# A second landing buffer for the sign-weight chunks at the start of a three-layer transformer kernel

## What is computed

```
Wb = sign(W_ffn)                                   # [1024, 1024]
x = x + 0.5 * einsum('bsi,oi->bso', layernorm(x), Wb)
x = x + linear_attention(layernorm(x))             # phi(t) = elu(t) + 1, 16 heads of 64
x = x + 0.5 * einsum('bsi,oi->bso', layernorm(x), Wb)
```

## Time and profile before

| | us |
|---|---|
| median of 2 runs | 2100.75 (2100.37 to 2101.12) |
| the profiled execution's own time | 2100.6 |
| span of its slowest core (core 3), first to last instruction | 2099.0 |
| spans of all eight cores | 2093.1 to 2099.0 |
| PE busy on core 3 | 1767.8 (84%) |
| ACT busy | 1233.5 (59%) |
| DVE busy | 759.8 (36%) |

### The profile page before, as it was taken

How to read it: one execution, slowest core, us unless ns; L and a number is a source line. 1 busy time by engine, 2 the same in 40 slices (tenths; PEclk the granted TensorE clock), 3 DMA queues, 4 the chain that set the end, 5 groups by cost and what they waited for, 6 DMA issues and landing times.

```text
span 2099.0 us, 33066 instructions; the slowest of 8 cores (2093.1 to 2099.0 us)
## 1 busy us (share of the span) xinstructions
PE 1767.8 (84%) x10784; PEld 793.0 (38%) x10784; DVE 759.8 (36%) x2049; ACT 1233.5 (59%) x2025; POOL 147.5 (7%) x274
## 2 busy tenths in 40 slices
PE   0289989989989989989899899778888888888887
PEld 0133333333333333333333333344444444444443
DVE  2033333333333333333333333134443443443443
ACT  1266766776766776766777766634444444444443
POOL 1000000000000001000000000011011011011010
PEclk9999999999999999999999999989999999999999
DMA  8612222222222223222222221123333333333332
GB/s 169 131 61 70 85 88 72 84 88 78 77 88 72 84 87 111 75 88 66 88 89 66 88 89 56 60 92 112 125 120 113 119 125 115 113 118 115 120 126 76
DMA packets 134630, 199.34 MB, mean 95 GB/s; under 512 B 88384, under 2 KB 88384, under 8 KB 134464
## 3 DMA queue, kind: packets, MB, share of 16 engines
q0 software_dynamic: 32960, 109.08, 16.0%
q1 hardware_dynamic: 101504, 88.15, 13.8%
HBM read 104.87 MB, written 83.89 MB: 90 GB/s over the span
## 4 chain that ended last, share of the span: by engine, by line
PE 54%; ACT 25%; issue 10%; DVE 6%; DMA 3%; ACTq 1%; DVEq 0%; SPq 0%
PE pA L463 34%; PE pA L474 12%; DVE y2t L341 4%; ACT u1b L442 3%; PE pA L468 3%; DMA stg<-wfT 3%; ACT mnb L397 3%; ACT mxb L399 3%; ACT u2b L448 3%; PE pA L478 2%; ACT nb L357 2%; ACT kbQ L385 2%; ACT eb L398 2%; PE tpB L453 2%; ACT kbQ L386 1%
## 5 line engine op out<-in xcount | busy, mean ns | idle before, releaser
L474 PE MATMUL pA<-wv,u1fm 128*128 128x512 bf16 x1024 | 245.3, 383 | 96.8 <-ACT kbK L401 96.8
L463 PE MATMUL pA<-sw,u2fm 128*128 128x512 bf16 x1024 | 234.6, 383 | 76.7 <-DVE y2t L341 75.5
L474 PE MATMUL pA<-wk,u1fm 128*128 128x512 bf16 x1024 | 242.4, 379 | 18.3 <-ACT kbQ L385 18.3
L442 ACT ACTIVATE u1b<-y2t 128x1024 bf16<-128x1024 f32 x64 | 67.6, 1057 | 299.5 <-DVE y2t L341 299.5
L463 PE MATMUL pA<-wo,attnfm 128*128 128x512 bf16 x1024 | 234.1, 382 | 4.9 <-DVE y3t L321 1.0
L463 PE MATMUL pA<-sw,u0fm 128*128 128x512 bf16 x1024 | 235.7, 384 | 0.0
L463 PE MATMUL pA<-wq,u1fm 128*128 128x512 bf16 x1024 | 232.1, 380 | 0.0
L474 PEld LDWEIGHTS pA<-wv,u1fm 128*128 128x128 bf16 x1024 | 90.9, 98 | 213.4 <-issue 123.8
L463 PEld LDWEIGHTS pA<-sw,u2fm 128*128 128x128 bf16 x1024 | 96.5, 98 | 194.7 <-issue 90.7
L382 ACT ACTIVATE u2b<-y1t 128x1024 bf16<-128x1024 f32 x63 | 66.6, 1057 | 175.9 <-DVE y1t L281 175.8
L312 DVE TENSOR_TENSOR phiQ<-eb,mxb 128x1024 bf16<-128x1024 bf16 x64 | 44.3, 693 | 344.0 <-ACT mxb L399 344.0
(11 more groups left out here) (119 smaller groups left out, 2418.1 us busy)
## 6 DMA issues: line engine op xcount, KB each, us to landing
xt<-x SPq DMA_DIRECT2D x64, 512.0 KB, 3.9
y1scr<-y1t POOLq DMA_DIRECT2D x64, 512.0 KB, 3.9
y1in<-y1scr POOLq DMA_DIRECT2D x64, 512.0 KB, 3.9
out<-y3t SPq DMA_DIRECT2D x64, 512.0 KB, 2.6
qscr<-qfm POOLq DMA_DIRECT2D x64, 256.0 KB, 3.2
qfin<-qscr POOLq DMA_DIRECT2D x64, 256.0 KB, 4.1
qfm<-phiQ SPq DMA_TRANSPOSE x512, 2.3
stg<-wfT SPq DMA_DIRECT2D x8, 512.0 KB, 8.6
```

The costliest lines, as they stand in the source:

```text
L442: e.activation(u1b[:, 0, :], y2t[:, tw % 2, :], AF.Square, accum_out=sq3b[:, :]).then_inc(sSq3, 1)
L463: mm = e.matmul(dst[:, h*512:(h+1)*512], lhs_fm[:, c*P:(c+1)*P], w_sb[:, c, h*512:(h+1)*512], start=(c == 0), stop=(last and c == 7))
L474: mm = e.matmul(dst[:, h*512:(h+1)*512], lhs_fm[:, c*P:(c+1)*P], w_sb[:, c, h*512:(h+1)*512], start=(c == 0), stop=(last and c == 7))
```

## The change

Chunks with an even number still land in `stg`, those with an odd number in `y3t[:, 0, :]`, which nothing else uses in this stage. SP's wait on `sSw` becomes c - 1 instead of c and begins at c = 2, so the buffer's last reader but one must be done. The wait on `gStg` is not changed: chunk c is issued only after chunk c - 1 has landed. ACT reads the buffer that fits.

```diff
             for c in range(8):
+                buf = stg[:, 0, :] if c % 2 == 0 else y3t[:, 0, :]
+                if c >= 2:
+                    e.wait_ge(sSw, c - 1)
                 if c >= 1:
-                    e.wait_ge(sSw, c)
                     e.wait_ge(gStg, 16 * c)
-                e.dma_start(out=stg[:, 0, :], in_=wfT[c*P:(c+1)*P, :]).then_inc(gStg, 16)
+                e.dma_start(out=buf, in_=wfT[c*P:(c+1)*P, :]).then_inc(gStg, 16)
@@
             for c in range(8):
                 e.wait_ge(gStg, 16 * (c + 1))
-                e.sign(sw[:, c, :], stg[:, 0, :]).then_inc(sSw, 1)
+                e.sign(sw[:, c, :], stg[:, 0, :] if c % 2 == 0 else y3t[:, 0, :]).then_inc(sSw, 1)
```

## The result

The changed kernel takes 2086.84 us (median), the kernel before 2101.4 us measured beside it. The ratio is 0.993, with a 95% interval of 0.9919 to 0.9941: 14.6 us less. The forecast was 2086 us in a range of 2081.5 to 2095.

What follows compares the result with a forecast made beforehand. Bound: eight serial `wfT` chunk loads ahead of PE's first work. Gaps 9.4 us, plus 6.1 for one slow transfer made fast, less a 0.5 tail, give 15.0 off 2100.6: 2086 us, range 2081.5 to 2095.

Steps and rivals of the forecast that it cites:

- Part 1: Gaps between chunk loads: ACT's sign no longer delays the next issue; gaps fall from 10.12 to 0.7 us, gain 9.4.
- Part 2: Start of the chunk loads: c2 gets in ahead of the weight loads, 6.1 us gained less a 0.5 us tail.
- Part 3: Chunks c3 to c7: c3 takes 11.21 us, the others 8.18 to 8.70; c7 lands at 66.8 us.
- Parts 4 to 6: Behind the chunks: no weight becomes the bound, the rest shifts as a block, core 4 ends last at 2084.3 us.
- The low stretch: PE's first tile: granted clock 0.62 over 97 to 106 us follows PE's pause; falling otherwise, at most 3.4 us either way.
- B: Rival: c2 does not get in ahead of the weight loads and takes 11.21 us; only gaps go, 2091 us; chance 0.14.
- C: Rival: full DMA engines stretch the transfers when gaps go, old cadence holds from c3; gain 9.2, 2091 us; chance 0.13.
- D: Rival: the shift makes granted-clock dips fall in three more slices, loss 20.4 us, 2106 us; chance 0.04.
- E: Rival: nothing happens, 2100.6 us, since the sign was not what held SP back; chance 0.05 shared with B with C.

Runs made afterwards that it cites:

- late_c3c7: Changed kernel with the new sign wait for c3 to c7 only, c1 and c2 keeping the old wait; ratio to the kernel before 0.9978.
- after_sign2b: Changed kernel with each chunk's sign taken twice, the second after the first; ratio to the kernel before 0.9939.
- before_hold3: Kernel before, with POOL's four weight loads held back until c2 has landed; ratio to the kernel before 0.9964.
- after_hold4: Changed kernel with the weight loads held until c3 has landed; ratio to the kernel before 0.9877.
- two_in_flight: Changed kernel without the wait for the landing just before, one landing semaphore per buffer, two transfers under way; 2065.47 us, ratio to the kernel before 0.9832.
- two_hold8: Changed kernel with two transfers under way and the weight loads held until all eight chunks have landed; 2071.38 us, ratio to the kernel before 0.9856.
- after_hold8: Changed kernel with the weight loads held until all eight chunks have landed; 2075.86 us, ratio to the kernel before 0.9882.

## Why the prediction was right

*What bounds.* Right: the eight chunks in series set PE's start, and what is behind shifts as a block (2013 to 2019 us before and after).

*Part 1, the sign leaves the cycle, 9.4 us.* Right. The semaphore's way to SP, taken as 0.1 us, is 0.07 to 0.08, so the seven gaps take 0.5 us where 0.7 were forecast. The half change late_c3c7 shows five of the seven gaps as 6.4 us against 5.8 expected, and after_sign2b shows that the sign has cover to spare.

*Part 2, c2 gets in ahead, 5.6 us.* Right, with c2 at 3.73 us against the 4.19 taken (3.69 and a tail of 0.5). The forecast said landing at 21.36 us; core 7's is at 21.45. That it is so near is in part luck: the tail of 0.5 us on c2 did not come, but c1 took 4.42 us where 3.69 were taken, and nothing on record says why. before_hold3 shows the mechanism by itself. One term failed in this step: "its bias loads are a few KB and share with one chunk before and after, so I leave 18.35 for `wq`". They are a few KB, but they go one after the other, beside the chunks, and on four cores they delay `wq` to 20.9 to 21.8 us. On those a second chunk is saved. It did not spoil the time, since the metric is the slowest core and the four others issue `wq` at 18.5 to 19.0; that some core stays without the delay was not part of the forecast. With the wait of after_hold4 on all cores the ratio is 0.9877. It does show in the mean, where the eighth sign is 17.0 us earlier and not 14 to 15.

*Part 3, the others keep their lengths.* Right on the whole: c3 11.12 us (11.21 taken), c4 to c7 34.6 us together (33.7). Of these 0.9 us 0.7 are left in the landing of c7 on core 7, at 67.5 where 66.8 was forecast; the shorter hops make up most of the rest.

*Parts 4 to 6.* Right, except for the core that ends last. `wv` lands on core 7 at 69.5 us (near 69) and is wanted at 103.48; PE waits for no weight. The low stretch moved with the tile, 0.62 over 82 to 91 us on core 7, and the slow sixteen products took 5.74 us (5.69 before). The forecast looked at cores 3 and 4; the slowest is core 7, and core 4, one of the four with a late `wq`, ends at 2077.7 and not at 2084.3. Core 3 ends at 2082.6 (2084.0 forecast).

*Rivals.* B did not come about on any core: c2's sign follows c1's by 3.7 to 4.1 us on all eight. C was refuted by late_c3c7: the transfers did not stretch. That agrees with what the Trainium skill says in "DMA: Bandwidth & Descriptors", section "Queues, rings and completion order", that a DMA engine goes round its queues a packet at a time, and two_in_flight fits it too, since a pair takes 9.5 to 11.0 us where one chunk takes 8.2 to 9.0; the rule itself was not isolated here. D did not come: the clocks after are 0.991 to 0.993, as before. A lower clock did appear in the runs in which PE has to wait for weights (0.987 to 0.991). E falls by the time, since the interval ends at 0.9941.

*The sum.* Slowest span forecast 2084.3, found 2085.2; with the 1.6 us outside the span 2085.9 and 2086.8. The statement that a change below 42 us can hardly be told from none did not hold: the 14.6 us are clear of noise, with an interval that is 2.3 us to either side.

## What to carry to other kernels

A wait that shows a large time in a queue's list is not worth that time when another wait stands behind the same event: here, beside 65.6 us on the sign, the gaps between transfers shrank by 9.6 us, and the change gave 14.6 in all; dropping the wait for the landing as well gave 36. When a short serial load shares the DMA engines with a bulk load that nobody needs yet, look at who is issued first; but hold the bulk load only as long as its own first user has slack, which two_hold8 and after_hold8 overran by 10 and 12 us. Small loads that are chained one behind the other set the start of everything that the same engine issues after them.

## What was not expected of the hardware

- Two 512 KB loads under way beside the weight loads take 9.5 to 11.0 us as a pair, one by itself 8.2 to 9.8 us and the first that meets them 8.5 to 11.2 us; without them one takes 3.6 to 4.4 us.
- A 2 KB load took 66.4 us behind four weight loads in the same queue, 1.7 us when that queue was free, and near 4 us beside a chunk in the other queue.
- In after_hold8, where PE has to pause for weights, the granted clock stayed at 0.68 to 0.89 over four stretches of 15 us, 55 to 115 us; in the first three the DMA share was 105 to 110%, in the last 16%. Whether the pauses or something else kept it low was not separated.
